# Row gathers of attention and pooling: written out one by one with indices taken from the slot table, and released by the sums themselves

## The chip, the core and the metric

The program runs on one core of one Trainium2 chip. The metric is the device time of one execution in microseconds (us), lower is better. The engines are TensorE (PE in the profile, its weight loads PEld), VectorE (DVE), ScalarE (ACT), GpSimd (POOL) and the DMA queues that SyncE (SP) and GpSimd feed.

## What is computed

A graph network on 3125 nodes of 256 features and 53125 edges (`src`, `dst`), in four parts. Two of them gather a row for each edge, and only they are touched:

```python
# part 1, three layers; each head of the source attends over the four heads of the target
scores = einsum('ehd,egd->ehg', Q[src], K[tgt]) / sqrt(DH)
msg = einsum('ehg,egd->ehd', softmax(scores), V[tgt]) + Ee[et]
hidden = relu(layer_norm(hidden + segment_sum(msg @ Wo.T + bo, src)))
# part 3, once
w = exp(-relu((a_s[:, src] + a_d[:, dst] + aw_e * elem + ab) / 20))
out = segment_sum(w * feats[dst], src) / segment_sum(w, src)
```

Parts 2 and 4 are expert layers and are not touched.

## The kernel before

The edges are sorted once by source and cut into tiles of up to 128 edges, one edge on each partition; the edges of a tile belong to few source nodes, so that sums over them fall in a window of 16 nodes. Four tiles (`BT`) are a batch, and there are 104 batches. The table `slot_dst` in SBUF holds, for each partition and tile, the row of the edge's target node. It is made before the layers and not changed after.

`attention_edges` runs once in each of the three layers (a hardware loop over the layers), and `pooling_edges` once. Both are a pipeline over the 104 batches, in which every engine has its own program and they meet in semaphores:

- GpSimd gathers the rows of a batch from DRAM into one of six sets of the buffer `kv` (`SETS`), by four indirect DMAs of 128 rows each: 2048 bytes a row in attention (keys and values), 1040 bytes in pooling (features and one dot product for each head).
- In attention TensorE does for batch b, in this order: the scores (4 matmuls that mark strangers, L1278, and 32 records of scores, L1287), the transposes of the keys of batch b+1 (8, L1269), and the weighted sums of batch b-2 (32, L1300), whose end counts up `sums_ready`. In pooling it does the scores of b (L2023, L2024) and then the sums of b-1 (48 records, L2033 and L2035).
- ScalarE copies the queries (`queries`), the transposed keys (`copies`), takes the exponent and makes the selection (`select`).
- VectorE takes maxima (L1221, and L1975 in pooling: one for each batch), makes the weights and adds the sums to the totals.

A set of `kv` is free for the gathers of batch b when the sums of batch b-6 are done. In the kernel before ScalarE waits for that: at the end of its step b, `destinations` waits for the sums of batch b-2, copies the four index columns of batch b+4 from `slot_dst` into a small tile `idx` with one set of columns for each set of `kv` (L1177, L1938), and counts up `idx_ready`. GpSimd waits for `idx_ready` and gathers with the indices in `idx`. The copy lets GpSimd's program be a hardware loop: `batches` writes out six steps, then loops over bodies of six, and the address of `idx` is the same in each turn. The first four batches of attention (one of pooling) are gathered ahead in the phase before, by `first_gathers` (L209), which already takes its indices from `slot_dst`. The gathers up to the sixth batch wait only for the first copy.

Of the kernel before, what the change touches and what calls it, by code (L numbers as in the profile page):

```python
# [12 lines left out]
P = 128  # L13
# [1080 lines left out]
def attention_edges(nc, t, sb, pb, g, layer):  # L1094
# [5 lines left out]
    with ExitStack() as st:  # L1100
        def s(name, shape, dt=F32):
            return sb("ae_" + name, shape, dt, st)
        idx = s("idx", (P, SETS, BT), I32)
        q = s("q", (P, FEW, BT, H, W))
# [12 lines left out]
        out_ps = pb(st, "out_ps", (P, 2, 512))  # L1117
        with phase(nc, "ae", "idx_ready", "turn", "q_ready", "sel_ready", "kT_ready", "kT_copied",
                   "scores_ready", "own_ready", "top_ready", "low_ready", "exp_ready", "z_ready", "rz_ready",
# [15 lines left out]
            @block.gpsimd  # L1135
            def _(pool):
                last_row = pool.to_reg(NP_ - 1)

                def step(b, n, k):

                    pool.wait_ge(m.idx_ready, b - SETS + 2 if after(b, SETS) else 1)
                    pool.sem_inc(m.turn, 1)
                    for u in range(BT):
                        pool.indirect_dma_start(  # L1144
                            kv[:, k, u, :], None, kv_d, bass.IndirectOffsetOnAxis(ap=idx[:, k, u:u + 1], axis=0),
                            bounds_check=last_row, oob_is_err=False).then_inc(loaded[k], 16)
                batches(pool, AHEAD, BATCHES, SETS, step)

            @block.scalar
            def _(act):  # L1150
# [20 lines left out]

                def destinations(b, k):

                    if after(b, 2) and (not isinstance(b, int) or b + SETS - 2 < BATCHES):
                        act.wait_ge(m.sums_ready, b - 1)
                        act.sem_inc(m.turn, 1)
                        act.activation(idx[:, (k - 2) % SETS, :], slot_dst[:, bass.ds((b + SETS - 2) * BT, BT)], ACT.Copy).then_inc(m.idx_ready, 1)  # L1177

                def step(b, n, k):
                    if not isinstance(b, int) or b + 1 < BATCHES:  # L1180
                        queries(b + 1, (k + 1) % SETS)
                        copies(b + 1)
                    act.wait_ge(m.low_ready, b + 1)
                    act.activation(ex[:, k % 2, :, :], low[:, k % 2, :, :], ACT.Exp).then_inc(m.exp_ready, 1)
                    if not isinstance(b, int) or b + 1 < BATCHES:
                        select(b + 1, (k + 1) % SETS)
                    destinations(b, k)
                act.activation(idx[:, :, :], slot_dst[:, 0:SETS * BT].rearrange("p (s u) -> p s u", u=BT), ACT.Copy).then_inc(m.idx_ready, 1)
                queries(0, 0)
# [680 lines left out]
def pooling_edges(nc, t, sb, pb, g):  # L1870
# [5 lines left out]
    with ExitStack() as st:  # L1876
        def s(name, shape, dt=F32):
            return sb("pe_" + name, shape, dt, st)
        idx = s("idx", (P, SETS, BT), I32)
        a_src = s("a_src", (3, FEW, BT, H, W), BF16)  # L1880
# [9 lines left out]
        sc_ps, out_ps = pb(st, "pe_sc", (P, 2, 512)), pb(st, "pe_out", (P, 2, 512))  # L1890
        with phase(nc, "pe", "loaded", "const_ready", "turn", "idx_ready", "src_ready", "edge_step",
                   "sel_ready", "scores_ready", "own_ready", "part_ready", "sum_ready", "low_ready", "exp_ready", "weights_ready",
                   "sums_ready", "added", ends=(loaded,)) as (block, m):

            @block.gpsimd
            def _(pool):
                last_row = pool.to_reg(NP_ - 1)

                def step(b, n, k):

                    pool.wait_ge(m.idx_ready, b - SETS + 2 if after(b, SETS) else 1)
                    pool.sem_inc(m.turn, 1)
                    for u in range(BT):
                        pool.indirect_dma_start(  # L1904
                            feat[:, k, u, :], None, f_d, bass.IndirectOffsetOnAxis(ap=idx[:, k, u:u + 1], axis=0),
                            bounds_check=last_row, oob_is_err=False).then_inc(loaded[k], 16)
                batches(pool, 1, BATCHES, SETS, step)

# [6 lines left out]
            def _(act):  # L1915
# [16 lines left out]

                def destinations(b, k):

                    if after(b, 2) and (not isinstance(b, int) or b + SETS - 2 < BATCHES):
                        act.wait_ge(m.sums_ready, b - 1)
                        act.sem_inc(m.turn, 1)
                        act.activation(idx[:, (k - 2) % SETS, :], slot_dst[:, bass.ds((b + SETS - 2) * BT, BT)], ACT.Copy).then_inc(m.idx_ready, 1)  # L1938

                def step(b, n, k):  # L1940
# [4 lines left out]
                    act.activation(ex[:, k % 2, :, :], low[:, k % 2, :, :], ACT.Exp, scale=-1.0).then_inc(m.exp_ready, 1)  # L1945
                    destinations(b, k)
                act.activation(idx[:, :, :], slot_dst[:, 0:SETS * BT].rearrange("p (s u) -> p s u", u=BT), ACT.Copy).then_inc(m.idx_ready, 1)
                sources(0, 0)
# [478 lines left out]
```

## Time and profile before

| | us |
|---|---|
| median of 3 runs (lowest, highest) | 5239.12 (5237.07, 5248.7) |
| profiled execution, its own time | 5233.94 |
| span of its trace | 5232.0 |
| GpSimd busy | 2424.9 (46%) |
| TensorE busy | 3759.6 (72%) |
| mean granted TensorE clock | 0.743 |

The span is the time from the first to the last instruction of the trace. A granted clock of 1.0 is 2.4 GHz, and 0.5 is 1.2 GHz; a value between is a mean over a stretch. A gather stands in the trace as DMA_INDIRECT on POOL: the time in which GpSimd makes its descriptors; the rows land later. `x4` behind a row counts instructions. In brackets stands the idle time of the engine before the instruction, and what the profile takes for its end; "issue" is time in which the engine waited for nothing that the profile shows.

### The profile page before, as it was taken

What the parts mean: (1) busy time and instruction counts of PE and PEld (TensorE: products, weight loads), DVE (VectorE), ACT (ScalarE), POOL (GpSimd) and SP (SyncE); (2) the same over time, 40 slices, a digit from 0 to 9 for tenths busy, and PEclk for the clock granted to TensorE, in tenths of its full rate; (3) what the DMA queues carried; (4) which work ended last, traced back from release to release, by engine and by line L of the source; (5) the groups of instructions that cost most, each with busy time, mean ns of one, the idle gap of its engine ahead of it and who ended that gap; (6) DMA issues with size and microseconds to landing.
All of it is one profiled execution on the core that took longest, in us unless ns stands there. A gap on an engine that the chain in (4) does not pass through costs nothing. (4 is left out here: it accounts for less than half of the span.)

```text
span 5232.0 us, 112793 instructions
## 1 busy us (share of the span) xinstructions
PE 3759.6 (72%) x36105; PEld 2965.2 (57%) x36105; DVE 2729.3 (52%) x8902; ACT 1515.5 (29%) x6308; POOL 2424.9 (46%) x2373
## 2 busy tenths in 40 slices
PE   4666554888888788888887888888856455555677
PEld 3444332677777557777764777776645344444566
DVE  7666665556556545565554566565424233333423
ACT  1222220433334133333323333332222111121122
POOL 2666565455555145555523555553035444444201
PEclk9985556888788888888888788787867555555579
DMA  1110004455555145555523455553047222222100
GB/s 61 41 41 17 1 1 135 127 143 144 141 140 144 45 125 143 141 143 142 144 59 114 129 144 143 145 143 95 31 140 139 67 65 65 65 65 65 32 26 20
DMA packets 209041, 493.57 MB, mean 94 GB/s; under 512 B 73145, under 2 KB 97301, under 8 KB 207880
## 3 DMA queue, kind: packets, MB, share of 16 engines
q0 software_dynamic: 149120, 429.71, 29.7%
q1 hardware_dynamic: 59799, 62.33, 3.9%
q8 instruction: 64, 1.05, 0.1%
q14 instruction: 58, 0.48, 0.0%
HBM read 430.59 MB, written 62.94 MB: 94 GB/s over the span
## 5 line engine op out<-in xcount | busy, mean ns | idle before, releaser
L1144 POOL DMA_INDIRECT kv<-kv_table,ae_idx x1200 | 1232.4, 1027 | 1017.5 <-ACT ae_idx L1177 702.8
L1287 PE MATMUL sc_ps<-ae_q,ae_kT 64*128 64x64 f32 x9984 | 802.0, 312 | 97.3 <-issue 95.8
L1287 PEld LDWEIGHTS sc_ps<-ae_q,ae_kT 64*128 64x128 f32 x9984 | 741.6, 222 | 211.1 <-issue 202.2
L1221 DVE TENSOR_REDUCE ae_own<-sc_ps 128x64 f32<-128x1024 f32 x312 | 382.1, 1225 | 734.8 <-PE sc_ps L1287 502.2
L1300 PE MATMUL out_ps<-hid,kv 128*64 128x64 f32 x9984 | 529.3, 264 | 114.4 <-issue 90.2
L1904 POOL DMA_INDIRECT kv<-feature_table,pe_idx x412 | 411.1, 998 | 423.8 <-ACT pe_idx L1938 313.3
L741 POOL DMA_INDIRECT edge_records<-rec_c,idx x416 | 422.7, 1016 | 352.9 <-ACT rec_c L501 224.2
L1300 PEld LDWEIGHTS out_ps<-hid,kv 128*64 128x64 f32 x9984 | 449.7, 173 | 211.8 <-issue 189.6
L1154 ACT ACTIVATE ae_kT<-kT_ps 128x512 f32<-128x512 f32 x624 | 365.1, 595 | 665.3 <-PE kT_ps L1269 487.3
L1205 DVE TENSOR_TENSOR totals<-totals,out_ps 128x32 f32 x2496 | 447.1, 179 | 209.9 <-DVE totals L1205 4.1
L2033 PE MATMUL pe_out<-pe_wgt,kv 128*64 128x16 f32 x3328 | 298.9, 264 | 309.4 <-issue 224.4
L1269 PE MATMUL kT_ps<-ident,kv 128*128 128x128 f32 x2496 | 469.6, 348 | 24.1 <-PEq L84 22.8
L2033 PEld LDWEIGHTS pe_out<-pe_wgt,kv 128*64 128x64 f32 x3328 | 276.8, 221 | 361.0 <-issue 293.6
L1252 DVE TENSOR_TENSOR hid<-ae_att,ae_sel 128x512 f32<-128x512 f32 x624 | 404.1, 689 | 0.2
L1269 PEld LDWEIGHTS kT_ps<-ident,kv 128*128 128x128 f32 x2496 | 370.2, 178 | 52.7 <-issue 25.9
L1278 PE MATMUL sc_ps<-marks,ident_big 128*128 (+1 forms) x1248 | 249.0, 305 | 120.0 <-issue 117.7
L1169 ACT ACTIVATE ae_q<-qT 128x32 f32 x1248 | 271.4, 217 | 191.9 <-issue 186.1
L1170 ACT ACTIVATE ae_q<-qT 128x32 f32 x1248 | 267.0, 214 | 0.1
L2035 PE MATMUL pe_out<-pe_wgt,pe_ones_f 128*64 128x32 f32 x1664 | 220.8, 291 | 46.9 <-issue 46.9
L1975 DVE TENSOR_REDUCE pe_own<-pe_sc 128x16 f32<-128x256 f32 x104 | 43.8, 421 | 397.1 <-DMA et_xs<-expert_in 397.1
L1970 DVE TENSOR_TENSOR pooled<-pooled,pe_out 128x32 f32 x832 | 157.1, 189 | 157.2 <-issue 78.1
L671 PE MATMUL same_ps<-hotT 50*128 50x128 bf16 x416 | 62.9, 304 | 212.5 <-ACT hotT L509 149.2
(448 smaller groups left out, 5736.8 us busy)
## 6 DMA issues: line engine op xcount, KB each, us to landing
kv<-kv_table,ae_idx POOLq DMA_INDIRECT x1200
et_w<-in_EW SPq DMA_DIRECT2D x56, 192.5 KB
expert_in<-kv SPq DMA_DIRECT2D x14, 512.0 KB
et_xs<-expert_in SPq DMA_DIRECT2D x56, 128.0 KB, 3.8
expert_out<-et_o POOLq DMA_DIRECT2D x56, 128.0 KB, 3.6
edge_records<-rec_c,idx POOLq DMA_INDIRECT x416
kv<-feature_table,pe_idx POOLq DMA_INDIRECT x412
nodes_placed<-kv SPq DMA_DIRECT2D x12, 512.0 KB
```

Of the source, the lines that this page charges most:

```text
L741: pool.indirect_dma_start(xy_d, bass.IndirectOffsetOnAxis(ap=idx[:, j, c:c + 1], axis=0), rec_c[:, j, c, :], None, bounds_check=last_row, ...
L1144: pool.indirect_dma_start(kv[:, k, u, :], None, kv_d, bass.IndirectOffsetOnAxis(ap=idx[:, k, u:u + 1], axis=0), bounds_check=last_row, oob ...
L1154: act.activation(kT[:, 2 * f:2 * f + 2, :, :], kT_ps[:, 2 * f:2 * f + 2, :, :], ACT.Copy).then_inc(m.kT_copied, 1)
L1169: act.activation(q[:, k % FEW, u, :, 0:WL], qT[:, :, bass.ds(rows[u], WL)], ACT.Copy).then_inc(m.q_ready, 1)
L1205: v.tensor_tensor(own_rows, own_rows, new, ALU.add).then_inc(m.added, 1)
L1221: v.tensor_reduce(own[:, j, :, :].rearrange("p g x -> p (g x)"), sc_ps[:, j, :, :, :].rearrange("p e i (x w) -> p (e i x) w", w=W), axis=A ...
L1252: v.tensor_tensor(wgt[:, jo, 2 * f:2 * f + 2, :, :], bc(att[:, jo, 2 * f:2 * f + 2, :, :].rearrange("p u g h -> p u (g h)"), 3, W), bc(sel ...
L1269: last = pe.transpose(kT_ps[:, u, i, :], kv[:, k, u, i * P:(i + 1) * P], ident[:, :])
L1287: last = pe.matmul(sc_ps[:, k % 2, e, i, u * HW:(u + 1) * HW], kT[rows, u, i, :], q[rows, k % FEW, u, :, :].rearrange("p h w -> p (h w)"), ...
L1300: last = pe.matmul(o[e * DH:(e + 1) * DH, :], kv[:, k, u, D + head * DH:D + (head + 1) * DH], wgt[:, k % 2, u, at * H:(at + 1) * H, :].rea ...
L1904: pool.indirect_dma_start(feat[:, k, u, :], None, f_d, bass.IndirectOffsetOnAxis(ap=idx[:, k, u:u + 1], axis=0), bounds_check=last_row, oo ...
L2033: pe.matmul(out_ps[rows, k % 2, at:at + W], feat[:, k, u, h * DH:(h + 1) * DH], wgt[:, k % 2, u, h, :], start=True, stop=True)
```

## The change

The tile `idx` and the semaphore `idx_ready` go, and with them `destinations` on ScalarE. GpSimd's loop over batches is written out in full (100 batches in attention, 103 in pooling), each gather takes its index column from `slot_dst` at a fixed address, and the first gather of a batch waits for the sums of the batch that used its set. The two functions are changed in the same way; of the second the GpSimd part is shown.

```diff
@@ attention_edges
-        idx = s("idx", (P, SETS, BT), I32)
...
-                def step(b, n, k):
-
-                    pool.wait_ge(m.idx_ready, b - SETS + 2 if after(b, SETS) else 1)
-                    pool.sem_inc(m.turn, 1)
+                for b in range(AHEAD, BATCHES):
+                    if b >= SETS:
+                        pool.wait_ge(m.sums_ready, b - SETS + 1)
                     for u in range(BT):
                         pool.indirect_dma_start(
-                            kv[:, k, u, :], None, kv_d, bass.IndirectOffsetOnAxis(ap=idx[:, k, u:u + 1], axis=0),
-                            bounds_check=last_row, oob_is_err=False).then_inc(loaded[k], 16)
-                batches(pool, AHEAD, BATCHES, SETS, step)
+                            kv[:, b % SETS, u, :], None, kv_d, bass.IndirectOffsetOnAxis(ap=slot_dst[:, b * BT + u:b * BT + u + 1], axis=0),
+                            bounds_check=last_row, oob_is_err=False).then_inc(loaded[b % SETS], 16)
...
-                def destinations(b, k):
-
-                    if after(b, 2) and (not isinstance(b, int) or b + SETS - 2 < BATCHES):
-                        act.wait_ge(m.sums_ready, b - 1)
-                        act.sem_inc(m.turn, 1)
-                        act.activation(idx[:, (k - 2) % SETS, :], slot_dst[:, bass.ds((b + SETS - 2) * BT, BT)], ACT.Copy).then_inc(m.idx_ready, 1)
...
-                    destinations(b, k)
-                act.activation(idx[:, :, :], slot_dst[:, 0:SETS * BT].rearrange("p (s u) -> p s u", u=BT), ACT.Copy).then_inc(m.idx_ready, 1)
@@ pooling_edges
+                for b in range(1, BATCHES):
+                    if b >= SETS:
+                        pool.wait_ge(m.sums_ready, b - SETS + 1)
                     for u in range(BT):
                         pool.indirect_dma_start(
-                            feat[:, k, u, :], None, f_d, bass.IndirectOffsetOnAxis(ap=idx[:, k, u:u + 1], axis=0),
-                            bounds_check=last_row, oob_is_err=False).then_inc(loaded[k], 16)
-                batches(pool, 1, BATCHES, SETS, step)
+                            feat[:, b % SETS, u, :], None, f_d, bass.IndirectOffsetOnAxis(ap=slot_dst[:, b * BT + u:b * BT + u + 1], axis=0),
+                            bounds_check=last_row, oob_is_err=False).then_inc(loaded[b % SETS], 16)
```

On GpSimd the attention stage of one layer is, before, as follows; `ae_idx` is the tile `idx` of attention, and L95 is the hardware loop, whose body is gone through 15 times.

```order
L1144 DMA kv<-kv_table,ae_idx 128x512 x24
L95 UNCONDITIONAL_BRANCH
L95 ISA
L1144 DMA kv<-kv_table,ae_idx 128x512 x4
L1141 REGISTER_ALU
L1144 DMA kv<-kv_table,ae_idx 128x512 x4
...
L95 REGISTER_ALU
L95 COMPARE_AND_BRANCH
L1144 DMA kv<-kv_table,ae_idx 128x512 x16
```

Of the changed kernel the same place is this, between the branches that enter and leave the stage.

```order
L1134 UNCONDITIONAL_BRANCH
L1142 DMA kv<-kv_table,slot_dst 128x512 x400
L81 UNCONDITIONAL_BRANCH
```

The loop and its registers are gone, and 400 gathers stand in a row; in pooling there are 412 of them. On ScalarE the end of one written-out step of attention, before, is this: exponent, selection, the copy of the indices, and then the registers of the next queries.

```order
L1184 ACTIVATE ae_ex<-ae_low 128x64
L1159 ISA
L1161 ISA
L1161 ACTIVATE ae_sel<-marks 128x64
L1177 ISA
L1177 ACTIVATE ae_idx<-slot_dst 128x4
L192 ISA
L192 TENSOR_LOAD tile_row
```

The two rows of L1177 are gone in the changed kernel, and the selection is followed by the registers.

## Rows read from the trace of the kernel before

**Rows 1.** Busy time by stage: attention of layer 1, and pooling

```profile
core 0: us, PE busy (x) PEld busy (x) DVE busy (x) ACT busy (x) POOL busy (x), PEclk, DMA share, GB/s
976.00:1724.00 748.00, 647.75 (x7752) 548.54 (x7752) 446.08 (x1618) 295.14 (x1329) 403.77 (x393) 0.80 0.50 139
...
4080.00:4915.00 835.00, 421.34 (x5090) 344.78 (x5092) 282.05 (x1520) 162.84 (x1101) 403.53 (x405) 0.50 0.24 65
```

**Rows 2.** First and last start of the maxima, one for each batch

```profile
L1221 DVE TENSOR_REDUCE ae_own<-sc_ps x104: 1218/1225/1226, 975.8 to 1724.7; 128x64 f32<-128x1024 f32 x104
...
L1975 DVE TENSOR_REDUCE pe_own<-pe_sc x104: 411/420/426, 4071.9 to 4913.1; 128x16 f32<-128x256 f32 x104
```

**Rows 3.** Costliest groups of the page: the gathers

```profile
L1144 POOL DMA_INDIRECT kv<-kv_table,ae_idx x1200 | 1232.4, 1027 | 1017.5 <-ACT ae_idx L1177 702.8
...
L1904 POOL DMA_INDIRECT kv<-feature_table,pe_idx x412 | 411.1, 998 | 423.8 <-ACT pe_idx L1938 313.3
```

**Rows 4.** Timeline: sums, index copy and gather where nothing is late

```profile
1503.18 2.02 PE L1300 MATMUL out_ps<-hid,kv 128*64 128x64 f32 x32
...
1505.79 0.20 ACT L1177 ACTIVATE ae_idx<-slot_dst 128x4 int32 x1
...
1506.78 1.16 POOL L1144 DMA_INDIRECT kv<-kv_table,ae_idx  x1 [2.79 <-ACT ae_idx L1177]
```

**Rows 5.** Busy time in four short stretches of attention

```profile
1335.31:1339.89 4.58, 4.58 (x78) 4.04 (x77) 3.86 (x13) 2.36 (x11) 2.89 (x3) 1.00 0.37 107
1343.70:1346.67 2.97, 2.84 (x45) 2.46 (x46) 2.67 (x11) 2.08 (x12) 2.36 (x3) 1.00 0.33 97
1346.67:1349.40 2.73, 0.89 (x6) 0.59 (x5) 1.78 (x5) 0.17 (x1) 2.11 (x2) 1.00 0.69 189
1351.09:1354.63 3.54, 3.54 (x41) 3.09 (x40) 2.91 (x13) 2.16 (x9) 2.67 (x3) 0.55 0.45 116
```

**Rows 6.** Timeline of the same batch: gathers and index copy

```profile
1343.70 0.99 POOL L1144 DMA_INDIRECT kv<-kv_table,ae_idx  x1 [1.88 <-ACT ae_idx L1177]
...
1347.60 1.49 POOL L1144 DMA_INDIRECT kv<-kv_table,ae_idx  x1 [0.30 <-issue]
...
1349.78 0.20 ACT L1177 ACTIVATE ae_idx<-slot_dst 128x4 int32 x1 [2.95 <-DMA node_types<-node_b]
...
1350.77 1.00 POOL L1144 DMA_INDIRECT kv<-kv_table,ae_idx  x1 [1.69 <-ACT ae_idx L1177]
```

**Rows 7.** Timeline of TensorE at the lower clock

```profile
1308.57 1.97 PE L1269 MATMUL kT_ps<-ident,kv 128*128 128x128 f32 x8
1310.46 1.98 PE L1300 MATMUL out_ps<-hid,kv 128*64 128x64 f32 x32
1312.37 1.03 PE L1278 MATMUL sc_ps<-marks,ident_big 128*128 x4
...
1320.66 3.68 PE L1287 MATMUL sc_ps<-ae_q,ae_kT 64*128 64x64 f32 x32
```

**Rows 8.** Busy time in three stretches of pooling, two batches

```profile
4397.69:4400.20 2.51, 2.49 (x46) 2.35 (x44) 1.21 (x9) 1.00 (x9) 1.99 (x2) 0.50 0.19 53
4400.20:4409.10 8.90, 2.45 (x10) 1.57 (x10) 1.18 (x6) 1.61 (x11) 5.99 (x6) 0.50 0.39 104
4409.10:4414.00 4.90, 3.47 (x50) 2.89 (x50) 3.14 (x17) 0.62 (x4) 0.00 (x1) 0.50 0.00 1
```

**Rows 9.** Timeline of the same two batches

```profile
4397.69 0.99 POOL L1904 DMA_INDIRECT kv<-feature_table,pe_idx  x1 [6.16 <-ACT pe_idx L1938]
...
4406.80 1.00 POOL L1904 DMA_INDIRECT kv<-feature_table,pe_idx  x1 [0.30 <-issue]
...
4409.35 0.42 DVE L1975 TENSOR_REDUCE pe_own<-pe_sc 128x16 f32<-128x256 f32 x1 [7.66 <-DMA et_xs<-expert_in]
...
4414.00 0.99 POOL L1904 DMA_INDIRECT kv<-feature_table,pe_idx  x1 [6.19 <-ACT pe_idx L1938]
```

**Rows 10.** Timeline: one of the written-out gathers of `first_gathers`

```profile
938.91 1.02 POOL L209 DMA_INDIRECT kv<-kv_table,slot_dst  x1 [0.30 <-issue]
```

More of the change, by code:

```diff
@@ L1117, in attention_edges @@
         out_ps = pb(st, "out_ps", (P, 2, 512))
-        with phase(nc, "ae", "idx_ready", "turn", "q_ready", "sel_ready", "kT_ready", "kT_copied",
+        with phase(nc, "ae", "turn", "q_ready", "sel_ready", "kT_ready", "kT_copied",
                    "scores_ready", "own_ready", "top_ready", "low_ready", "exp_ready", "z_ready", "rz_ready",
@@ L1878, in s @@
             return sb("pe_" + name, shape, dt, st)
-        idx = s("idx", (P, SETS, BT), I32)
         a_src = s("a_src", (3, FEW, BT, H, W), BF16)
@@ L1890, in pooling_edges @@
         sc_ps, out_ps = pb(st, "pe_sc", (P, 2, 512)), pb(st, "pe_out", (P, 2, 512))
-        with phase(nc, "pe", "loaded", "const_ready", "turn", "idx_ready", "src_ready", "edge_step",
+        with phase(nc, "pe", "loaded", "const_ready", "turn", "src_ready", "edge_step",
                    "sel_ready", "scores_ready", "own_ready", "part_ready", "sum_ready", "low_ready", "exp_ready", "weights_ready",
@@ L1897, in _ @@
                 last_row = pool.to_reg(NP_ - 1)
-                def step(b, n, k):
-                    pool.wait_ge(m.idx_ready, b - SETS + 2 if after(b, SETS) else 1)
-                    pool.sem_inc(m.turn, 1)
+                for b in range(1, BATCHES):
+                    if b >= SETS:
+                        pool.wait_ge(m.sums_ready, b - SETS + 1)
                     for u in range(BT):
                         pool.indirect_dma_start(
-                            feat[:, k, u, :], None, f_d, bass.IndirectOffsetOnAxis(ap=idx[:, k, u:u + 1], axis=0),
-                            bounds_check=last_row, oob_is_err=False).then_inc(loaded[k], 16)
-                batches(pool, 1, BATCHES, SETS, step)
+                            feat[:, b % SETS, u, :], None, f_d, bass.IndirectOffsetOnAxis(ap=slot_dst[:, b * BT + u:b * BT + u + 1], axis=0),
+                            bounds_check=last_row, oob_is_err=False).then_inc(loaded[b % SETS], 16)
             @block.sync
@@ L1931, in sources @@
                                            ACT.Copy).then_inc(m.src_ready, 1)
[L1933 to L1938, printed above, removed]
                 def step(b, n, k):
@@ L1945, in step @@
                     act.activation(ex[:, k % 2, :, :], low[:, k % 2, :, :], ACT.Exp, scale=-1.0).then_inc(m.exp_ready, 1)
-                    destinations(b, k)
-                act.activation(idx[:, :, :], slot_dst[:, 0:SETS * BT].rearrange("p (s u) -> p s u", u=BT), ACT.Copy).then_inc(m.idx_ready, 1)
                 sources(0, 0)
```

## The prediction

> **What bounds the kernel now.** I read the stages first. An attention stage takes (1724.7 - 975.8) / 103 = 7.27 us a batch, pooling (4913.1 - 4071.9) / 103 = 8.17 us [rows 2]. Three attention stages and pooling are thus some 3080 us of the span of 5232. In attention TensorE is busy 648 of 748 us at a granted clock of 0.80; in pooling only 421 of 835, and at 0.50 throughout [rows 1]. GpSimd is busy for about half of either, and its groups of gathers show where it idles: mostly for ScalarE's index copy, 702.8 and 313.3 us [rows 3]. That idle time would cost nothing by itself: rows are gathered four batches ahead, and no row here shows TensorE waiting for them.
>
> The short stretches show what does cost. With nothing in its way TensorE does a whole batch in 4.58 us at 2.4 GHz. Four gathers start at 1343.70, and in that batch TensorE does 45 matmuls in the first 2.97 us, and then only 6 in 2.73 us, still at the full clock [rows 5]. It goes on at 1349.40, 0.31 us after the last of the four gathers ended (1347.60 + 1.49) [rows 6]. ScalarE is dry in the same time: its index copy comes at 1349.78, 0.38 us after TensorE resumes and after 2.95 us of idling, and the next gathers start at 1350.77 [rows 6]. So a burst of gathers starves the engines of instructions from about 3 us after its start until just after its end; the engine has some 45 matmuls in store and gets a trickle beyond. At 1.2 GHz the same burst costs nothing: 3.54 of 3.54 us busy while the next four gathers run, mean clock 0.55 [rows 5]. A batch at that clock takes 1.89 + 1.91 + 0.97 for transposes, sums and marks (start to start) and about 3.61 for the scores, 8.4 us [rows 7]. The clock fell right behind the dry stretch of 1346.67 to 1349.40 [rows 5].
>
> Pooling is worse. Two batches of gathers run as one burst of eight, from 4397.69 to 4407.80, and the next starts at 4414.00: 16.31 us for two batches [rows 9]. TensorE does 46 matmuls in the first 2.5 us, 10 in the next 8.9, and 50 in the 4.9 us after 4409.10, which is 1.3 us behind the last gather [rows 8]. VectorE too stood 7.66 us before L1975 and went on at 4409.35 [rows 9].
>
> **ScalarE's part of the change.** It loses one copy of 0.20 us a batch [rows 4] and its wait. I cost that at nothing: ScalarE is busy 295 of 748 us [rows 1], and its work for TensorE (queries, transposed keys) is done a step ahead. If that cover were missing, it would be at most 0.20 x 415 = 83 us to the good.
>
> **GpSimd's written-out code.** A gather that reads `slot_dst` at a fixed address takes 1.02 us with 0.30 before it [rows 10], the same as one with `idx` (mean 1027 ns, 0.30 before it) [rows 3, 6]. So nothing by instruction. GpSimd's instructions now come from straight code, fetched while its own gathers run; bounds: zero, or up to one burst's worth of delay, hidden by the lead of four batches. The Trainium skill (Runtime: NRT & Kernel Launch, Instruction fetch mechanics) says that a taken branch breaks the sequential prefetch and that unrolled code is preferred, which would be a small gain; no row here shows a cost of the loop's branch.
>
> **The release of the gathers.** This is what counts, since it moves the bursts. Where nothing is late, sums end at 1505.20, the copy starts at 1505.79, and the gather at 1506.78, 1.58 us after the sums and 0.79 after the copy [rows 4]. The changed GpSimd sees the sums itself: I take 0.8 us from sums to gather, as from copy to gather; the bounds are 0.3 (the gap inside a burst) and 1.2. More important, a copy that is itself starved, as at 1349.78, no longer holds the next burst until the one before has ended: the cycle gathers, dry ScalarE, copy, gathers took 1350.77 - 1343.70 = 7.07 us [rows 6], near the 7.27 of a batch, and it goes.
>
> At 2.4 GHz the new cycle is: sums end, 0.8 us in which TensorE does the marks and a few scores; 45 more matmuls from the store, which brings it through the scores and transposes and into the sums; dry until 4.9 + 0.4 us after the start of the burst, some 6 matmuls; the remaining 16 sums, 0.5 us. Together 0.8 + 4.9 + 0.4 + 0.5 = 6.6 to 6.7 us. Only then are the next gathers released, so that bursts stay apart. What is it today at this clock? A granted clock of 0.80 is 40% of the time at 1.2 GHz. From 0.4 / 8.4 + 0.6 / y = 1 / 7.27 the fast batch is y = 6.7 us. So the stall is not shorter, only at a fixed place: among the dense sums, not in the scores, as at 1346.67, where the clock fell after it. What is gained depends on how much less often the clock falls. I take half as often: 0.2 / 8.4 + 0.8 / 6.7 = 1 / 7.0, 0.27 us a batch, and over 3 x 104 batches 84 us. Bounds: nothing (share unchanged), and 170 to 240 us (hardly any low clock; release 0.3 us after the sums).
>
> In pooling the dry time of a burst is its length + 1.3 - 2.5 us: 8.9 us for eight gathers, 4.9 + 1.3 - 2.5 = 3.7 for four. The free time needed is (16.31 - 8.9) / 2 = 3.7 us a batch. With bursts of four a batch takes 7.4 us, and 8.17 - 7.4 over some 98 batches is 75 us. But a batch is about 50 matmuls, and store and trickle give nearly as many within a burst of four: sums can end just before the burst does, and then two bursts join as now. I take two batches of three apart: 50 us.
>
> Sum: 84 + 50 = 134 us off the profiled execution's 5234, which is 5100; the median of the runs shown is 5 us higher, so about 5100 to 5105. I forecast 5100.
>
> **The rule that speaks against it.** What the rows show is told above: matmuls fall from 45 in 2.97 us to 6 in 2.73 us while gathers run [rows 5]. The Trainium skill (SBUF — State Buffer, Who interferes with whom) says "DMA never contends with a compute engine". By that the place of the gathers would be of no matter, and the time would stay 5239. The trace does not agree; it is the first rival.
>
> **Rivals.**
> - The moved bursts change nothing on balance: each burst costs its dry stretch wherever it stands, there are as many as before, and the clock falls as often. For it: y above is the same before and after. Against it: the joined bursts of pooling. The time is 5239, or down to 5200 when only a little comes of pooling. Chance 0.24, of which 0.10 within 0.2%.
> - Bursts join in attention as they do in pooling: the end of the next sums comes before the burst's end, and GpSimd, which ScalarE no longer holds back, starts eight gathers in a row. A burst of eight is dry for 10.1 + 0.4 - 3 = 7.5 us, two of four for 2 x 2.3 = 4.6: 1.45 us a batch more. It decides if more than about a quarter of the fast batches join: at a quarter, 0.25 x 200 x 1.45 = 73 us eats what pooling gives; at two thirds it is 190, less 50, and 5380. For it: now the sums often end inside the burst, so that the next set is free at once. Against it: from the release to the burst's end TensorE gets through some 60 matmuls (8 before the burst, 45 and 6 within) and a batch has 76. Chance 0.18.
> - More than forecast: release in 0.3 us and a clock that hardly falls: 170 to 240 in attention and 75 in pooling, 4920 to 4990. Chance 0.08, within the range for the most part.
> - The forecast, 5000 to 5200: chance 0.50.
>
> **Chances and range.** A measurement tells about 0.2% (10 us) from no change. Faster: 0.50 + 0.08 + 0.14 = 0.72; within 0.2%: 0.10; slower 0.18. The range is 4950 to 5250: it leaves out some 0.15 above and 0.05 below.
>
> **What would show it.** In the trace after: gathers start 0.3 to 1.2 us after the end of L1300's run; bursts of four in attention, with TensorE's dry stretch in the sums; a granted clock in the attention stages above 0.85 and 7.0 us from maximum to maximum; bursts of four in most of pooling and 7.5 to 7.7 us a batch. The forecast is wrong if bursts of eight appear in attention, if the clock stays at 0.80 there, or if pooling keeps its pairs with 16.3 us.

## The result, and the profile after

The changed kernel takes 4945.9 us (median of 4 runs, 4937.03 to 4952.88) against 5241.56 for the kernel before (4 runs): a ratio of 0.9438, with a 95% interval of [0.9417, 0.9458]. That is 296 us less, and 154 below the 5100 that were forecast. The profiled execution took 4947.18 us, its span is 4945.3 and its mean granted clock 0.78.

The first and last start of the maxima give the pace again, in attention of layer 1 and in pooling (in the changed kernel L1221 is L1209, and L1975 is L1951):

```profile
L1209 DVE TENSOR_REDUCE ae_own<-sc_ps x104: 1216/1224/1226, 981.0 to 1687.5; 128x64 f32<-128x1024 f32 x104
...
L1951 DVE TENSOR_REDUCE pe_own<-pe_sc x104: 417/424/426, 3980.4 to 4627.4; 128x16 f32<-128x256 f32 x104
```

Attention takes 706.5 / 103 = 6.86 us a batch (6.91 and 6.94 in the other two layers; 7.27, 7.22 and 7.26 before), pooling 647.0 / 103 = 6.28 (8.17 before, [rows 2]). Over 103 batches that is 107 us from the three attention stages and 194 us from pooling: all of the gain, and most of it from the stage from which 50 us were expected.

Busy time by stage (attention of layer 1, pooling), and in two short stretches around one burst of gathers in attention:

```profile
core 0: us, PE busy (x) PEld busy (x) DVE busy (x) ACT busy (x) POOL busy (x), PEclk, DMA share, GB/s
980.00:1688.00 708.00, 561.96 (x7779) 469.69 (x7781) 446.47 (x1620) 271.60 (x1229) 397.72 (x392) 0.95 0.52 147
3980.00:4628.00 648.00, 394.94 (x5114) 320.58 (x5115) 291.45 (x1533) 151.53 (x1031) 419.75 (x411) 0.50 0.31 85
1403.60:1406.60 3.00, 2.95 (x40) 2.64 (x40) 2.34 (x14) 1.09 (x7) 2.39 (x3) 1.00 0.42 111
1406.60:1409.60 3.00, 1.31 (x28) 1.03 (x30) 1.17 (x3) 0.85 (x6) 1.32 (x2) 1.00 0.65 187
```

The granted clock of attention rose from 0.80 [rows 1] to 0.95 (0.93 and 0.91 in layers 2 and 3). The dry stretch of TensorE is still there. In the timeline of the same place it stands in the sums, as forecast: only two of the 32 come between 1407.25 and 1409.03, and the rest follow 0.8 us after the last gather (1407.23 + 1.00) has ended. The next gather starts at 1410.23, 0.3 us after the sums.

```profile
1403.32 1.00 POOL L1142 DMA_INDIRECT kv<-kv_table,slot_dst  x1 [1.66 <-PE out_ps L1288]
...
1406.80 0.45 PE L1288 MATMUL out_ps<-hid,kv 128*64 128x64 f32 x7 [0.25 <-issue]
1407.23 1.00 POOL L1142 DMA_INDIRECT kv<-kv_table,slot_dst  x1 [0.30 <-issue]
1407.56 0.29 PE L1288 MATMUL out_ps<-hid,kv 128*64 128x64 f32 x2 [0.31 <-issue]
1409.03 0.93 PE L1288 MATMUL out_ps<-hid,kv 128*64 128x64 f32 x23 [1.18 <-issue]
1410.23 1.00 POOL L1142 DMA_INDIRECT kv<-kv_table,slot_dst  x1 [2.01 <-PE out_ps L1288]
```

The costliest groups say it for the whole span: the idle time with no releaser ("issue") now stands before the sums (L1288), 389.8 us. In the kernel before it was spread over the scores (L1287), the sums (L1300) and the marks (L1278), and it was less, 303.7 us in all:

```profile
L1287 PE MATMUL sc_ps<-ae_q,ae_kT 64*128 64x64 f32 x9984 | 802.0, 312 | 97.3 <-issue 95.8
L1300 PE MATMUL out_ps<-hid,kv 128*64 128x64 f32 x9984 | 529.3, 264 | 114.4 <-issue 90.2
L1278 PE MATMUL sc_ps<-marks,ident_big 128*128 (+1 forms) x1248 | 249.0, 305 | 120.0 <-issue 117.7
```

Of the changed kernel:

```profile
L1142 POOL DMA_INDIRECT kv<-kv_table,slot_dst x1200 | 1223.9, 1020 | 917.7 <-PE out_ps L1288 617.3
L1288 PE MATMUL out_ps<-hid,kv 128*64 128x64 f32 x9984 | 552.1, 240 | 423.2 <-issue 389.8
...
L1275 PE MATMUL sc_ps<-ae_q,ae_kT 64*128 64x64 f32 x9984 | 690.5, 293 | 16.6 <-ACT ae_kT L1151 16.6
...
L1890 POOL DMA_INDIRECT kv<-feature_table,slot_dst x412 | 420.9, 1022 | 220.4 <-DMA kv<-kv_table,slot_dst 118.5
```

So TensorE doesn't idle less in attention, it idles more. In layer 1 that idle time went from 99.9 to 139.7 us while the stage became 42 us shorter: all of attention's gain is the clock. The granted clock fell to 1.2 GHz 47 times in that stage before and 9 times after, and the share of the time spent there went from 0.40 to 0.11.

In pooling the pairs are gone: 98 of 99 bursts are of four gathers, where before 45 of 54 were of eight. The sums that the next burst waits for end at 4300.4, before the current burst's last gather, so by the forecast the two had to join. They don't: the next gather comes 1.19 us after the last one's end, and so it goes at every batch (0.99 to 1.34 us).

```profile
4299.93 0.45 PE L2011 MATMUL pe_out<-pe_wgt,pe_ones_f 128*64 128x32 f32 x3
...
4302.51 1.01 POOL L1890 DMA_INDIRECT kv<-feature_table,slot_dst  x1 [0.30 <-issue]
...
4304.71 1.00 POOL L1890 DMA_INDIRECT kv<-feature_table,slot_dst  x1 [1.19 <-DMA kv<-kv_table,slot_dst]
```

GpSimd itself is thus close to the bound of pooling: 4 x 1.00 + 3 x 0.30 + 1.2 = 6.1 of the 6.28 us.

### The profile page after: what moved, and what is told of

Same layout as the page of the kernel before. It is cut to its first block and busy times, and to the rows that moved or that the text cites. A ratio compares the mean times of both kernels' runs of the same rounds, so it can differ in the third digit from the quotient of the medians.

```text
span 4945.3 us, 110710 instructions
## 1 busy us (share of the span) xinstructions
PE 3520.7 (71%) x36105; PEld 2744.9 (56%) x36105; DVE 2734.3 (55%) x8902; ACT 1428.1 (29%) x5904; POOL 2426.0 (49%) x2373
## 3 DMA queue, kind: packets, MB, share of 16 engines
q0 software_dynamic: 149120, 429.71, 31.0%
## 5 line engine op out<-in xcount | busy, mean ns | idle before, releaser
L1142 POOL DMA_INDIRECT kv<-kv_table,slot_dst x1200 | 1223.9, 1020 | 917.7 <-PE out_ps L1288 617.3
L1288 PE MATMUL out_ps<-hid,kv 128*64 128x64 f32 x9984 | 552.1, 240 | 423.2 <-issue 389.8
L1288 PEld LDWEIGHTS out_ps<-hid,kv 128*64 128x64 f32 x9984 | 429.2, 148 | 573.2 <-issue 528.8
L1209 DVE TENSOR_REDUCE ae_own<-sc_ps 128x64 f32<-128x1024 f32 x312 | 381.9, 1224 | 633.3 <-DMA nodes_placed<-rows,node_pos 585.3
L1275 PE MATMUL sc_ps<-ae_q,ae_kT 64*128 64x64 f32 x9984 | 690.5, 293 | 16.6 <-ACT ae_kT L1151 16.6
L1275 PEld LDWEIGHTS sc_ps<-ae_q,ae_kT 64*128 64x128 f32 x9984 | 645.7, 205 | 90.9 <-ACT ae_kT L1151 48.0
L1151 ACT ACTIVATE ae_kT<-kT_ps 128x512 f32<-128x512 f32 x624 | 340.3, 594 | 713.9 <-remote 595.8
L1890 POOL DMA_INDIRECT kv<-feature_table,slot_dst x412 | 420.9, 1022 | 220.4 <-DMA kv<-kv_table,slot_dst 118.5
L1257 PE MATMUL kT_ps<-ident,kv 128*128 128x128 f32 x2496 | 375.9, 298 | 28.3 <-PEq L84 28.3
L2009 PEld LDWEIGHTS pe_out<-pe_wgt,kv 128*64 128x64 f32 x3328 | 251.3, 223 | 225.8 <-issue 186.3
L1257 PEld LDWEIGHTS kT_ps<-ident,kv 128*128 128x128 f32 x2496 | 295.6, 151 | 52.6 <-issue 29.8
L2011 PEld LDWEIGHTS pe_out<-pe_wgt,pe_ones_f 128*64 128x64 f32 x1664 | 200.1, 222 | 70.8 <-issue 70.0
L1174 ACT ACTIVATE ae_ex<-ae_low 128x64 f32<-128x64 f32 x312 | 80.0, 256 | 454.5 <-DVE ae_low L1227 444.8
```

The source lines that it names most:

```text
L1142: pool.indirect_dma_start(kv[:, b % SETS, u, :], None, kv_d, bass.IndirectOffsetOnAxis(ap=slot_dst[:, b * BT + u:b * BT + u + 1], axis=0), ...
L1151: act.activation(kT[:, 2 * f:2 * f + 2, :, :], kT_ps[:, 2 * f:2 * f + 2, :, :], ACT.Copy).then_inc(m.kT_copied, 1)
L1209: v.tensor_reduce(own[:, j, :, :].rearrange("p g x -> p (g x)"), sc_ps[:, j, :, :, :].rearrange("p e i (x w) -> p (e i x) w", w=W), axis=A ...
L1257: last = pe.transpose(kT_ps[:, u, i, :], kv[:, k, u, i * P:(i + 1) * P], ident[:, :])
L1275: last = pe.matmul(sc_ps[:, k % 2, e, i, u * HW:(u + 1) * HW], kT[rows, u, i, :], q[rows, k % FEW, u, :, :].rearrange("p h w -> p (h w)"), ...
L1288: last = pe.matmul(o[e * DH:(e + 1) * DH, :], kv[:, k, u, D + head * DH:D + (head + 1) * DH], wgt[:, k % 2, u, at * H:(at + 1) * H, :].rea ...
```

## The experiments

The theory: engines run dry in a burst of gathers; what counts is where a burst stands, how long it is, and how soon it is released. The rivals: the straight code or the table of slots does it; the early release alone does it, whatever the bursts' length; bytes moved starve the engines and not the gathers as such.

**One half at a time, and the release apart from the code (chip 7; the kernel before takes 5302.21 us there, 13 runs).** att_only and pool_only make the change in one function only. The changed kernel itself was not run on this chip. held_sep has the written-out code and `slot_dst`, but ScalarE's wait and copy stay, and GpSimd waits for them (its lines against the changed kernel):

```diff
-                        pool.wait_ge(m.sums_ready, b - SETS + 1)
+                        pool.wait_ge(m.idx_ready, b - SETS + 2)
+                    pool.sem_inc(m.turn, 1)
```

sep is the changed kernel with `pool.sem_inc(m.turn, 1)` between the wait and the gathers, so that the wait is an instruction of its own, as before, and not a part of the first gather.

> Only attention is changed; pooling is as before. Theory (the gathers' release sets where the bursts stand, each stage by itself): the three attention stages keep the 0.35 us a batch that the changed kernel's trace shows (7.25 to 6.90), about 109 us, and pooling keeps bursts of eight at 8.17 us a batch. 5125 to 5140. Rival (the stages help each other, or the gain is in common work such as ScalarE's lighter load): pooling gains too, and the time is under 5100.

> Only pooling is changed; attention is as before. Theory: pooling goes from 8.17 to about 6.28 us a batch, 195 us, attention stays at 7.25: 5040 to 5055. Both parts apart then add up to the 295 us measured together. Rival: as for attention alone.

> Gathers written out with indices from the slot table as in the change, but still released by ScalarE, which makes its copy of the indices as before (nobody reads it); between the wait and the gathers GpSimd counts up a semaphore, as before. Theory (the release is what counts): 5220 to 5260, no different from before, bursts of eight in pooling. Rival (straight code, or the index from the table, is the gain): 4945 to 5000.

> The changed kernel, with one more instruction: between the wait for the sums and the gathers GpSimd counts up a semaphore that nobody reads, so that the wait stands in an instruction of its own and not in the first gather. In the changed kernel's pooling the gap between two bursts is 1.2 us although the awaited sums ended some 3 us before the earlier burst did. Theory A (a gather that itself carries a wait cannot be prepared behind the one before it, and this gap keeps the bursts apart): the gap falls to 0.3 us, bursts join, pooling goes back towards 8 us a batch and attention joins some: 5100 to 5250. Theory B (GpSimd is itself short of instructions behind a burst): the gap stays at 1.2 us, and the time at 4945.

| | us, median | ratio [95%] | attention, us a batch | pooling |
|---|---|---|---|---|
| att_only | 5257.99 | 0.993 [0.9902, 0.9957] | 7.21, 7.24, 7.17 | 8.24 |
| pool_only | 5118.01 | 0.9659 [0.9633, 0.9685] | 7.35, 7.38, 7.33 | 6.39 |
| held_sep | 5298.64 | 0.9991 [0.9975, 1.0006] | 7.28, 7.31, 7.39 | 8.24 |
| sep | 5085.87 | 0.958 [0.9535, 0.9626] | 7.08, 7.23, 7.30 | 6.66 |

The code and the table are worth nothing by themselves (0.9991): without the new release nothing is gained. Pooling gives 184 us here and attention 44. Attention gives less than the 107 us of the first result because the clock recovers less: the stages of att_only still pass 31 to 34% of the time at 1.2 GHz, with 28 falls of the clock in layer 1, against 38 to 41% and 47 falls in held_sep. In sep a part of pooling's bursts joins, 24 of eight beside 48 of four, and it takes 0.27 us a batch more than pool_only. A separate wait also releases later: where a gather really had to wait for the sums it starts 0.8 us behind them, against 0.27 us in att_only, where the gather carries the wait. Here is one gap that stayed and one burst that joined the next (1.01 + 0.30 without a break), on GpSimd:

```profile
4321.10 0.99 POOL L1892 DMA_INDIRECT kv<-feature_table,slot_dst  x1 [1.70 <-DMA kv<-kv_table,slot_dst]
...
4325.00 1.01 POOL L1892 DMA_INDIRECT kv<-feature_table,slot_dst  x1 [0.30 <-issue]
4326.32 1.00 POOL L1892 DMA_INDIRECT kv<-feature_table,slot_dst  x1 [0.30 <-issue]
```

So the joining that was forecast exists with a separate wait. In the first result and in pool_only, where the gather carries the wait, a break of 1.0 to 1.4 us stood between any two bursts of pooling.

**Length of the bursts, and nearly no gathers (chips 10 and 2).** eights makes bursts of eight by waiting before every second batch only; pairs_att and pairs_b cut attention's bursts in two, with a wait for work of TensorE before the third gather; one_gather issues one gather of four and lets it count for all four, so that three quarters of the rows are stale and the output isn't the reference's; after_again and after_b are the changed kernel itself.

```diff
 eights, both functions
-                    if b >= SETS:
-                        pool.wait_ge(m.sums_ready, b - SETS + 1)
+                    if b >= SETS and (b % 2 == 0 or b == SETS):
+                        pool.wait_ge(m.sums_ready, min(b - SETS + 2, BATCHES))
 pairs
+                        if u == 2 and b >= SETS:
+                            pool.wait_ge(m.kT_ready, 2 * b - 2)
 one_gather
-                    for u in range(BT):
+                    for u in range(BT if b < SETS else 1):
```

> The changed kernel itself, for its time beside the others of this call, which may run on another chip than the first result. Between 0.940 and 0.962 of the kernel before; pooling at 6.2 to 6.4 us a batch in bursts of four.

> The changed kernel, but only every second batch waits, for the sums that free two sets, so that GpSimd issues eight gathers in a row in attention and in pooling. Theory (a burst starves the engines from about 3 us after its start to its end and a little more, so one long burst costs more than two short ones): a burst of eight is dry for 10.1 + 0.6 - 3 = 7.7 us, two of four for 5.0; attention 6.9 + 1.35 = 8.2 us a batch, pooling back at about 8, together 3 x 104 x 1.35 + 104 x 1.7 = 600 us slower than the changed kernel, at least 350 if the clock makes up for some. Rival (only the number of gathers counts, not how they are grouped): within 50 us of the changed kernel.

> The changed kernel, but in attention the third gather of a batch waits once more, for the transposes that come some 3.5 us after the sums that the first waits for: two bursts of two gathers (2.3 us) a batch. Theory: a burst of 2.3 us ends before TensorE's store of some 45 matmuls is used up, so nothing runs dry: 4.6 us of TensorE's work a batch, but GpSimd's 4 x 1.3 us and its gaps behind a wait become the bound, 6.0 to 6.4 us a batch. Three stages of 104 batches give 150 to 280 us: 4670 to 4800 where the changed kernel takes 4946, and the granted clock above 0.9 or low because TensorE waits for rows. Rival (the store does not fill in the short gap): no gain, or slower.

> The changed kernel, but from the seventh batch on only the first of the four gathers of a batch is issued, which counts for all four; three quarters of the rows are left from earlier batches, so this leaves out part of the computation. Theory: a burst of one never starves the engines; attention falls to TensorE's 4.6 us a batch at 2.4 GHz (3 x 104 x 2.3 = 700 us) and pooling to VectorE's 4.3 us (200 us): 4000 to 4150. Rival (the engines are short of instructions for another reason, such as TensorE's own loop): attention stays above 6 us a batch, over 4700.

> The changed kernel again, since the last call's chip showed no dry stretches in either kernel (kernel before 4216 us there, 5242 and 5302 us on the two chips before it). Where the kernel before takes over 5200 us: ratio 0.940 to 0.962, bursts of four in pooling at 6.2 to 6.4 us a batch. Where it takes about 4216 us: no difference.

> Gathers in bursts of eight in both stages (every second batch waits, for the sums that free two sets). On a chip with dry stretches, theory (dry from about 3 us after a burst's start to just behind its end): attention 8.2 us a batch, pooling about 8, at least 350 us slower than the changed kernel, so slower than the kernel before too. Rival (only the number of gathers counts): within 50 us of the changed kernel. On a chip without: no difference, as the last call showed.

> Attention in bursts of two gathers, the third gather waiting for the transposes. On a chip with dry stretches, theory (2.3 us of gathers do not use up TensorE's store): 6.0 to 6.4 us a batch in attention, 150 to 280 us less than the changed kernel. Rival (the store does not fill again in the short gap between two bursts): no gain, or slower.

> One gather a batch from the seventh batch on, three quarters of the rows left from earlier batches, which leaves out part of the computation. On a chip with dry stretches, theory: they are gone, attention at 5.0 and pooling at 4.35 us a batch, the same as the 3983 us that this kernel took on the chip without, to within 50 us. Rival (the slow chip starves the engines for another reason than the gathers): attention over 6 us a batch and 4600 us or more.

| | chip 10: us, ratio [95%] | chip 2: us, ratio [95%] |
|---|---|---|
| before | 4215.75 | 4216.63 |
| after | 4210.57, 0.998 [0.9962, 0.9999] | 4214.77, 0.9988 [0.997, 1.0006] |
| eights | 4222.92, 1.001 [0.9992, 1.0028] | 4227.95, 1.003 [1.001, 1.0051] |
| pairs | 4213.56, 0.9987 [0.9968, 1.0006] | 4213.53, 0.9999 [0.9983, 1.0016] |
| one_gather (one run) | 3982.82 | 3976.77 |

No one had expected this: on these chips the kernel before takes 4216 us, a fifth less than where the change was measured first, and the change is worth next to nothing (0.1 and 0.2%). Pace and busy time of after_b by stage:

```profile
L1209 DVE TENSOR_REDUCE ae_own<-sc_ps x104: 1216/1224/1226, 833.7 to 1393.8; 128x64 f32<-128x1024 f32 x104
...
L1951 DVE TENSOR_REDUCE pe_own<-pe_sc x104: 414/417/425, 3353.8 to 3890.2; 128x16 f32<-128x256 f32 x104
```

```profile
834.00:1394.00 560.00, 496.28 (x7776) 432.28 (x7775) 444.57 (x1620) 269.53 (x1229) 419.94 (x396) 0.96 0.67 187
3354.00:3890.00 536.00, 349.91 (x5102) 290.22 (x5102) 288.58 (x1529) 150.97 (x1027) 410.78 (x411) 0.50 0.38 102
```

Attention runs at 5.44 us a batch and pooling at 5.21, which is four gathers at 1.00 + 0.30: GpSimd gathers without a break (392 gathers in one row in attention) and is the bound. These gathers carry their waits as in the first result, but follow in 0.30 us here: no break of 1 us stands before them. The timeline shows TensorE at full pace beside them, waiting only for rows:

```profile
1102.86 1.03 POOL L1142 DMA_INDIRECT kv<-kv_table,slot_dst  x1 [0.30 <-issue]
1103.87 1.09 PE L1257 MATMUL kT_ps<-ident,kv 128*128 128x128 f32 x8 [0.34 <-DMA kv<-kv_table,slot_dst]
1104.20 1.00 POOL L1142 DMA_INDIRECT kv<-kv_table,slot_dst  x1 [0.30 <-issue]
1104.89 1.15 PE L1288 MATMUL out_ps<-hid,kv 128*64 128x64 f32 x32
1105.50 0.99 POOL L1142 DMA_INDIRECT kv<-kv_table,slot_dst  x1 [0.31 <-issue]
```

There is no dry stretch at all: TensorE's idle time with no releaser is 0.2 us in attention of layer 1. When a burst begins, how long it is and when it is released can't matter then, and these eight runs say nothing on the theory but that. The bursts of two were thus never tried where engines run dry.

**Again, and half the bytes (chip 12, which was of the same kind; then chip 6, which was not).** half_rows fetches 1024 bytes a row in attention in place of 2048, and other rows, so that its output isn't the reference's:

```diff
-                            kv[:, b % SETS, u, :], None, kv_d, ...
+                            kv[:, b % SETS, u, 0:D], None, kv_d.rearrange("n (two d) -> (n two) d", two=2), ...
```

> The changed kernel once more, as the anchor for the other kernels of this call. Theory D: where the kernel before takes some 5240 to 5300 us, its engines run dry in the gathers, and the change gives 0.94 to 0.95 of it, 6.9 us a batch in attention and 6.3 in pooling. Where the kernel before takes some 4216 us nothing runs dry, and the ratio is 1.00. Rival theory: the gain depends on neither, and any chip may give any ratio.

> The changed kernel, with GpSimd waiting only before every second batch, for the sums that free two sets, so that gathers run in bursts of eight by construction. Theory A (the length of a burst decides, where engines run dry): pooling goes back from 6.3 to about 8.2 us a batch, all of the 195 us that it had gained, and attention from 6.9 to 7.6 or more (a burst of eight is dry for 7.5 us against 2 x 2.3), so at least 200 us above the changed kernel on a chip where the kernel before takes over 5200. Theory B (the gain comes from the earlier release, whatever the length): within 60 us of the changed kernel. On a chip where the kernel before takes some 4216 us both give 1.00 to 1.005.

> The changed kernel, but in attention each gather fetches half a row, 1024 bytes in place of 2048, and from other rows; the values' half of the buffer stays stale, so the attention output isn't the reference's. As many gathers, descriptors and instructions as before, half the bytes. Where engines run dry: if the bytes moved starve them, the dry stretch shrinks and attention falls from 6.9 to below 6.3 us a batch; if the making or the number of the descriptors does, attention stays at 6.8 to 6.9. Where nothing runs dry (4216 us before) attention is bound by GpSimd and stays at 5.4, or falls to 5.2 if the rows' landing set it.

Chip 12: before 4214.86; after_c 4211.18 (0.999 [0.9972, 1.0008]), eights_c 4216.04 (1.0016 [0.9997, 1.0035]), half_rows_c 4206.19 (one run).

> As eights_c, which met a chip without dry stretches: GpSimd waits only before every second batch, for the sums that free two sets, so that gathers run in bursts of eight. Theory A (the length of a burst decides, where engines run dry): on a chip where the kernel before takes over 5200 us, pooling back at about 8.2 us a batch and attention at 7.6 or more, a ratio of 0.99 to 1.03 to the kernel before. Theory B (the earlier release, whatever the length): 0.94 to 0.955, as the changed kernel had on the first chip. Where the kernel before takes some 4216 us both give 1.00 to 1.005.

> The changed kernel, but from the seventh batch on only one of the four gathers of a batch is issued, so that three quarters of the edges use stale rows and the output isn't the reference's. It shows the rest of the kernel with hardly any gathers. On a chip where the kernel before takes over 5200 us: if the gathers alone make it slower than the 4216 us of the other chips, 3980 to 4100 us, as one_gather had there; if the chip is slower in everything, over 4500.

> As half_rows_c: in attention each gather fetches 1024 bytes of a row in place of 2048, and from other rows, so that the attention output isn't the reference's. Where engines run dry: attention below 6.3 us a batch if the bytes moved starve them, 6.8 to 6.9 if the making or the number of the descriptors does. Where nothing runs dry 4206 us, as before.

Chip 6 (the changed kernel itself was not run on it): before 5243.34 (7 runs); eights_d 5780.71 (1.104 [1.0998, 1.1082]); one_gather_d 4169.7 and half_rows_d 4926.68, one run each. The maxima of attention in eights_d, one_gather_d and half_rows_d, and those of pooling in eights_d and half_rows_d, whose pooling is that of the changed kernel:

```profile
L1209 DVE TENSOR_REDUCE ae_own<-sc_ps x104: 1217/1225/1226, 982.1 to 1928.6; 128x64 f32<-128x1024 f32 x104
...
L1951 DVE TENSOR_REDUCE pe_own<-pe_sc x104: 417/420/426, 4689.7 to 5446.6; 128x16 f32<-128x256 f32 x104
```

```profile
L1209 DVE TENSOR_REDUCE ae_own<-sc_ps x104: 1216/1218/1226, 982.2 to 1497.7; 128x64 f32<-128x1024 f32 x104
```

```profile
L1209 DVE TENSOR_REDUCE ae_own<-sc_ps x104: 1218/1225/1226, 975.0 to 1680.0; 128x64 f32<-128x1024 f32 x104
...
L1951 DVE TENSOR_REDUCE pe_own<-pe_sc x104: 418/425/426, 3960.5 to 4606.9; 128x16 f32<-128x256 f32 x104
```

*eights_d*: attention takes 9.19 us a batch against 6.86 in the first result and 6.84 in half_rows_d, pooling 7.35 against 6.28 in both. A longer burst undoes the change and much more, so the early release alone (theory B, 0.94 to 0.955) is out. Both sizes of theory A were off: attention lost three times what was expected, pooling half. In attention the dry time by itself came out as expected: TensorE's idle time with no releaser is 4.4 us for a burst of eight (214.8 us in 49 bursts of layer 1) against 1.4 for one of four (139.7 in 98), (214.8 - 139.7) / 103 = 0.73 us a batch more. Most of the rest of the 2.33 us is the clock, with 0.53 of the time at 1.2 GHz against 0.11. The short stretches of one burst of eight (1396.70 to 1407.50):

```profile
982.00:1929.00 947.00, 721.56 (x7776) 614.53 (x7778) 447.04 (x1620) 278.33 (x1229) 421.52 (x393) 0.74 0.38 110
4690.00:5447.00 757.00, 396.20 (x5108) 322.51 (x5110) 286.45 (x1530) 150.84 (x1026) 411.24 (x411) 0.50 0.27 72
1396.70:1402.50 5.80, 5.39 (x76) 4.43 (x73) 3.05 (x9) 1.29 (x8) 4.58 (x5) 0.87 0.46 130
1402.50:1408.27 5.77, 1.60 (x7) 0.78 (x7) 2.34 (x9) 1.97 (x11) 4.09 (x4) 0.72 0.66 188
```

76 matmuls, then 7 in 5.77 us. The store isn't always 45: here it lasted one whole batch. The granted clock fell within the dry stretch, at 1405.0, and came back at 1415.2. TensorE thus had nearly all of the second batch to do at 1.2 GHz before the next release: the gap to the next burst is 8.4 us here.

```profile
1406.51 0.99 POOL L1142 DMA_INDIRECT kv<-kv_table,slot_dst  x1 [0.30 <-issue]
1415.89 1.42 POOL L1142 DMA_INDIRECT kv<-kv_table,slot_dst  x1 [8.38 <-PE out_ps L1288]
```

*one_gather_d*: attention at 5.00 us a batch, the same as on chip 10 (5.00), and the whole at 4169.7 against 3977 to 3983 there. So TensorE and VectorE of such a chip are as quick in attention with hardly any gathers; it is the gathers that slow them. Of the 187 to 193 us that are left, 147 lie ahead of the first maximum (982.2 against 835.0 on chip 10), a part that gathers edge records and was not altered.

*half_rows_d*: 705.0 / 103 = 6.84 us a batch in each of the three layers with half the bytes, against 6.86, 6.91 and 6.94 for the changed kernel. Contrary to what was said before the run, the transfers were not as many: the page counts 110720 packets on the queue of the gathers against 149120, 32 fewer for each of attention's 1200 gathers. So neither the bytes nor the packets moved starve the engines. What stayed is GpSimd's work on a gather (mean 1009 ns against 1020); that this work, the making of the descriptors, is to blame is argued from what is left, and not shown.

## Why the prediction was wrong in size

**The mechanism** held in the first result: a burst starves the engines until just after its end, attention keeps bursts of four (98 of 98), and the dry stretch goes into the sums. The store ran out a little later than forecast, 3.9 us after the start of the burst shown above (1403.32 to 1407.25), and 5.8 us after the start of the burst of eight. eights_d shows that the length of the bursts decides, and held_sep that without the new release nothing changes.

**ScalarE's part and the written-out code** were put at nothing. For the code and the table held_sep shows it (0.9991). No run takes ScalarE's copy away and leaves the release as it was, so for the copy it is not shown.

**Attention, 84 us.** Measured 107. The release came 0.3 us after the sums (taken 0.8, lower bound 0.3). The fast batch of 6.7 us held: a clock of 0.95 is 10 to 11% of the time at 1.2 GHz, and 0.11 / 8.4 + 0.89 / y = 1 / 6.86 gives y = 6.7. The share of the low clock, taken at 0.2, was 0.11, 0.15 and 0.19 in the three stages. It was a guess, and that it came out near was luck: on chip 7 the share stays above 0.3 and attention gives 44 us, and in half_rows_d on chip 6 it is 0.09 to 0.10. Why the clock falls less often when the dry stretch stands in the sums no run shows.

**Pooling, 50 us.** Measured 194. This is the step that failed, and in two places: the slow release was left in the sum, and a third of the bursts was taken to join.

- "The free time needed is (16.31 - 8.9) / 2 = 3.7 us a batch" was kept for the changed kernel, though it holds the slow release. I gave attention the early release and forgot it here. In the trace before, the last sums of the pair end at 4411.66, the index copy stands behind an exponent that waits 9.80 us for VectorE, and the gather starts at 4414.00, 2.3 us after the sums (the median over that stage is 2.46 us):

```profile
4411.17 0.49 PE L2035 MATMUL pe_out<-pe_wgt,pe_ones_f 128*64 128x32 f32 x3
...
4412.81 0.21 ACT L1945 ACTIVATE pe_ex<-pe_low 128x16 f32<-128x16 f32 x1 [9.80 <-DVE pe_low L1996]
4413.00 0.20 ACT L1938 ACTIVATE pe_idx<-slot_dst 128x4 int32 x1
...
4414.00 0.99 POOL L1904 DMA_INDIRECT kv<-feature_table,pe_idx  x1 [6.19 <-ACT pe_idx L1938]
```

  In eights_d, with bursts of eight and the new release, it comes 0.3 us after them, as in all 49 bursts of that stage:

```profile
5010.12 0.45 PE L2011 MATMUL pe_out<-pe_wgt,pe_ones_f 128*64 128x32 f32 x3
...
5010.84 1.00 POOL L1890 DMA_INDIRECT kv<-feature_table,slot_dst  x1 [4.12 <-PE pe_out L2011]
```

  From 8.17 to the 7.35 us of eights_d are 103 x 0.82 = 84 us for the release (two chips, on which the kernel before takes 5242 and 5243 us).
- "I take two batches of three apart". All came apart, and from 7.35 to 6.28 are 110 us for that (both on chip 6); 84 + 110 is the 194 measured. The condition for joining was met (the awaited sums end 3.1 us before the burst does), and in sep 48 of 98 batches stand in joined bursts. In the changed kernel each first gather came 1.0 us or more behind the one before it, and this kept the bursts apart; the prediction had no such gap in its sum.

The earlier release is worth 2.2 us for each pair of batches by the medians (2.46 against 0.27), so 1.1 a batch, and 0.8 by the paces. Taken out of the 3.7 us of free time, the prediction's own sum gives 6.3 to 6.6 us a batch for bursts of four, all apart, where 6.28 was measured. Its dry time was thus sound; that it comes so near is partly luck, since GpSimd's own 6.1 us stand just below.

**The rivals.** "The moved bursts change nothing" named the wrong reason for the right thing on three chips: 0.998, 0.9988 and 0.999, since no engine runs dry there and GpSimd's own pace is the bound. The rule from the Trainium skill (SBUF — State Buffer, Who interferes with whom), that DMA never contends with a compute engine, agrees with the traces of chips 10, 2 and 12. Taken to mean that gathers cost the engines nothing, it does not agree with those of the first result and of chips 7 and 6. "Bursts join in attention" did not happen in the changed kernel; its price of 1.45 us a batch was too low, since forced bursts of eight cost 9.19 - 6.86 = 2.33, of which 0.73 is dry time and most of the rest the lower clock. "More than forecast" was nearest, but took pooling at its ceiling of 75 us, which rested on the same free time.

**What stays open.** Why engines run dry in a burst on some chips and not on others. The records of a gather (1.0 us, 0.30 between two) are alike on both kinds, and nothing that they hold tells the two apart. Each chip was met at one time only, so it isn't shown either whether this belongs to the chip or to its state at that time. That bytes and packets are not to blame is shown by one run with half of either; which resource the gathers take is not.

And why the first gather of a batch comes 1.0 to 1.4 us late in pooling. That it carries its wait can't be the whole reason, since the same kernel's gathers follow in 0.30 us at every batch on chips 10, 2 and 12. There, though, the awaited sums had ended 17 us and more before, against 4.3 us in the first result, and no run separates the chip from that lead.

## What to carry to other kernels

When a wait is moved, apply the new release in every stage that has it, and read in each how long the old path took from event to start: in pooling it was 2.3 us and not 0.8. Look at what the clock does and not only at the idle time: attention gained while TensorE idled more. Where engines idle with no releaser beside indirect DMAs, the length of a burst is a price of its own, to be tried by forcing it longer; eight in a row in place of four cost 2.3 us a batch in attention and 1.1 in pooling. And a stall that no record explains may not be there on another chip: measure such a change on several before it counts as won.

## What the runs showed of the hardware that was not expected

- The kernel before takes 4215 to 4217 us on chips 10, 2 and 12, and 5242 to 5302 in the first result and on chips 7 and 6. The changed kernel with three quarters of the gathers left out takes 3977 to 3983 on chips 10 and 2, and 4170 on chip 6.
- Of eight gathers in a row the first 5.8 us cost TensorE little (76 matmuls), the rest nearly everything (7 in 5.77 us); of four, 9 in the 2.2 us from 1406.80 to 1409.03.
- A gather that carries its wait starts 0.27 us after the sums that it waits for (att_only), one behind a separate wait 0.8 us (sep), both on chip 7.
- In the first result and on chips 7 and 6 pooling's first gather of a batch, which carries a wait for sums that ended 4.3 us before, starts 1.0 to 1.4 us after the gather before it; on chips 10, 2 and 12 the same gather starts after 0.30 us. With a separate wait (chip 7) some joined at 0.30 us (24 bursts of eight beside 48 of four), and the others came after 1.6 us or more.
- In attention of layer 1 TensorE's idle time with no releaser rose from 99.9 to 139.7 us and the stage still became 42 us shorter, because the clock fell 9 times and not 47.
- A gather of 128 rows takes 1.0 us and 0.30 to the next, with 2048, 1040 or 1024 bytes a row (means of 1020, 1022 and 1009 ns in the changed kernel and half_rows_d).
